# Third norm's scalar steps on GpSimd in place of VectorE, in a fused decoder layer

## The reference

```
x = x + attn(layernorm(x))      # q, k, v, o projections with LoRA, then a gated MLP
x = x + xattn(layernorm(x), ctx, ctx)
x = x + ffn(layernorm(x))

layernorm(x) = (x - mean(x)) / sqrt(var(x) + 1e-5)

xattn(Q, K, V):                 # per sequence and head
    corr = ifft(fft(q) * conj(fft(k))).real
    w, idx = top_k(corr, 8);  w = softmax(w)
    out = sum_i w_i * v[min(idx_i + pos, L - 1)]

ffn(x):                         # one of 8 LoRA experts for each token
    logits = x @ route_w.T;  best = top_1(logits)
    out = (one_hot(best) * logit)[..., None] * (x @ A.T) @ Bw
```

## Time and profile before

| | |
|---|---|
| median of 3 runs | 811.79 us |
| profiled execution, own time | 812.52 us |
| its span, first to last instruction | 810.3 us |
| TensorE busy | 753.6 us, 93% |
| VectorE busy | 563.3 us, 70% |
| ScalarE busy | 420.7 us, 52% |
| GpSimd busy | 242.3 us, 30% |
| mean granted TensorE clock | 0.983 |

### The profile page before, as it was taken

One profiled execution on the slowest core, in us unless ns is written; L12 is line 12 of the kernel. 1 busy time (PEld: TensorE's weight loads), 2 busy tenths in 40 slices (PEclk: granted clock), 3 DMA queues, 4 the chain that ended last, 5 costly groups with the idle time before them and its releaser, 6 DMA issues.

```text
span 810.3 us, 10362 instructions
## 1 busy us (share of the span) xinstructions
PE 753.6 (93%) x3256; PEld 532.3 (66%) x3256; DVE 563.3 (70%) x1291; ACT 420.7 (52%) x759; POOL 242.3 (30%) x196
## 2 busy tenths in 40 slices
PE   3979999999999999999999999999997778999975
PEld 1335778777888888888888888887774233444432
DVE  5998874567897477557637647752346689999983
ACT  7794753655664354345445435431132456777651
POOL 0001221033363343243343334321111142444441
PEclk9999999999999999999999999999999899999997
DMA  7463210012323023112302301120231535556301
GB/s 208 147 247 135 73 52 1 1 40 66 117 79 105 14 65 104 40 37 81 90 14 81 102 14 55 49 72 2 65 82 49 133 93 153 157 157 170 105 26 40
DMA packets 31286, 67.27 MB, mean 83 GB/s; under 512 B 4800, under 2 KB 5184, under 8 KB 31232
## 3 DMA queue, kind: packets, MB, share of 16 engines
q1 hardware_dynamic: 31232, 66.60, 27.6%
HBM read 45.61 MB, written 4.19 MB: 61 GB/s over the span
## 4 chain that ended last, share of the span: by engine, by line
PE 65%; issue 14%; DVE 9%; POOL 8%; ACT 3%; DMA 1%; SPq 0%; POOLq 0%; DVEq 0%; ACTq 0%
PE ps L667 19%; PE ps L669 19%; PE ps L668 19%; POOL pn L1120 5%; POOL en L1069 2%; PE ps L638 1%; POOL pw L850 1%; DMA lb<-in_lora_attn_b 1%; DVE piece_d L393 1%; DVE piece_c L389 1%; PE ps L463 1%; PE ps L462 1%; PE ps L693 1%; PE ps L898 1%; DVE odd_c L389 1%
## 5 line engine op out<-in xcount | busy, mean ns | idle before, releaser
L667 PE MATMUL ps<-x_hi,w_hi 128*128 128x512 f32 x448 | 176.2, 393 | 0.2 <-POOL w_lo L524 0.2
L669 PE MATMUL ps<-x_hi,w_lo 128*128 128x512 f32 x448 | 174.7, 390 | 0.0
L668 PE MATMUL ps<-x_lo,w_hi 128*128 128x512 f32 x448 | 174.3, 389 | 0.0
L783 POOL TENSOR_TENSOR h_lo<-hf,h_hi 128x512 fp32r<-128x512 f32 x56 | 74.0, 1321 | 244.5 <-ACT h_hi L778 244.4
L792 DVE TENSOR_TENSOR acc<-acc,ps 128x512 f32<-128x512 f32 x112 | 76.3, 684 | 73.1 <-PE ps L669 73.1
L771 DVE TENSOR_TENSOR hf<-hf,ps 128x512 f32<-128x512 f32 x56 | 38.4, 686 | 86.9 <-PE ps L669 86.9
L667 PEld LDWEIGHTS ps<-x_hi,w_hi 128*128 128x128 f32 x448 | 84.1, 188 | 21.6 <-issue 4.0
L524 POOL TENSOR_TENSOR w_lo<-wt,w_hi 128x512 fp32r<-128x512 f32 x42 | 62.4, 1486 | 113.8 <-ACT w_hi L517 113.8
L669 PEld LDWEIGHTS ps<-x_hi,w_lo 128*128 128x128 f32 x448 | 84.1, 188 | 18.0
L668 PEld LDWEIGHTS ps<-x_lo,w_hi 128*128 128x128 f32 x448 | 84.2, 188 | 17.3
L667 PE MATMUL ps<-w_hi,h_hi 128*128 128x512 f32 x224 | 88.1, 393 | 2.6 <-DVE acc L718 1.4
(11 more groups left out here) (153 smaller groups left out, 1324.9 us busy)
## 6 DMA issues: line engine op xcount, KB each, us to landing
codes_sb<-in_codes SPq DMA_DIRECT2D x40, 256.0 KB, 2.9
scale_sb<-in_scale_rows SPq DMA_DIRECT2D x80, 128.0 KB, 2.8
kc<-ku SPq DMA_DIRECT2D x64, 128.0 KB, 3.3
kx<-ku SPq DMA_DIRECT2D x32, 256.0 KB, 3.6
lft<-in_lora_ft SPq DMA_DIRECT2D x14, 512.0 KB, 4.3
acc<-in_x SPq DMA_DIRECT2D x4, 1024.0 KB, 8.2
ctx<-in_ctx SPq DMA_DIRECT2D x16, 256.0 KB, 4.9
out<-fin SPq DMA_DIRECT2D x16, 256.0 KB, 4.2
```

Of the source, the lines that this page charges most:

```text
L667: nc.tensor.matmul(bank, hi, rhs_hi, start=start, stop=False)
L668: nc.tensor.matmul(bank, hi, rhs_lo, start=False, stop=False)
L669: return nc.tensor.matmul(bank, lo, rhs_hi, start=False, stop=stop)
L783: nc.gpsimd.tensor_tensor(h_lo[:, c % 2, i], hf[:, i], h_hi[:, c % 2, i].bitcast(F32), ALU.subtract).then_inc(hlo_done, 1)
```

## The change

The four VectorE functions are gone, and GpSimd makes the same values behind its power, tile by tile. [...] Each waits for the step before it by the semaphore scaled3, which now counts six for a tile; the two waits on it (in dve_stats and in act_normalise_x3) change their numbers with it. In GpSimd's piece the two functions stand last in the slot, behind pool_pow.

```diff
@@ dve_stats
-            dve.wait_ge(scaled3, 4 * (t - 1))
+            dve.wait_ge(scaled3, 6 * (t - 1))
@@
-    def dve_square(dve, t, b):
-        dve.wait_ge(pow3, t + 1)
-        nc.vector.tensor_tensor(na3[:, b], pw3[:, b], pw3[:, b], ALU.mult).then_inc(scaled3, 1)
-
-    def dve_residual(dve, t, b):
-        dve.wait_ge(scaled3, 4 * t + 1)
-        nc.vector.scalar_tensor_tensor(out=nb3[:, b], in0=na3[:, b], scalar=-0.5, in1=ve3[:, b],
-                                       op0=ALU.mult, op1=ALU.mult).then_inc(scaled3, 1)
-
-    def dve_rstd(dve, t, b):
-        dve.wait_ge(scaled3, 4 * t + 2)
-        nc.vector.scalar_tensor_tensor(out=rs3[:, b], in0=nb3[:, b], scalar=1.5, in1=pw3[:, b],
-                                       op0=ALU.add, op1=ALU.mult).then_inc(scaled3, 1)
-
-    def dve_shift(dve, t, b):
-        dve.wait_ge(scaled3, 4 * t + 3)
-        nc.vector.scalar_tensor_tensor(out=nm3[:, b], in0=mv3[:, b, 0:1], scalar=-1.0, in1=rs3[:, b],
-                                       op0=ALU.mult, op1=ALU.mult).then_inc(scaled3, 1)
+    def pool_rstd(pool, t, b):
+        pool.wait_ge(pow3, t + 1)
+        nc.gpsimd.tensor_tensor(na3[:, b], pw3[:, b], pw3[:, b], ALU.mult).then_inc(scaled3, 1)
+        pool.wait_ge(scaled3, 6 * t + 1)
+        nc.gpsimd.tensor_tensor(nb3[:, b], na3[:, b], ve3[:, b], ALU.mult).then_inc(scaled3, 1)
+        pool.wait_ge(scaled3, 6 * t + 2)
+        nc.gpsimd.tensor_scalar(na3[:, b], nb3[:, b], -0.5, 1.5, ALU.mult, ALU.add).then_inc(scaled3, 1)
+        pool.wait_ge(scaled3, 6 * t + 3)
+        nc.gpsimd.tensor_tensor(rs3[:, b], na3[:, b], pw3[:, b], ALU.mult).then_inc(scaled3, 1)
+
+    def pool_shift(pool, t, b):
+        pool.wait_ge(scaled3, 6 * t + 4)
+        nc.gpsimd.tensor_tensor(nb3[:, b], mv3[:, b, 0:1], rs3[:, b], ALU.mult).then_inc(scaled3, 1)
+        pool.wait_ge(scaled3, 6 * t + 5)
+        nc.gpsimd.tensor_scalar(nm3[:, b], nb3[:, b], -1.0, None, ALU.mult).then_inc(scaled3, 1)
@@ act_normalise_x3
-        act.wait_ge(scaled3, 4 * (t + 1))
+        act.wait_ge(scaled3, 6 * (t + 1))
@@ GpSimd's piece
                 if a := at(4):
                     pool_pow(pool, *a[:2])
+                if a := at(4):
+                    pool_rstd(pool, *a[:2])
+                if a := at(4):
+                    pool_shift(pool, *a[:2])
@@ VectorE's piece, behind dve_hidden
-                if a := at(5):
-                    dve_square(dve, *a[:2])
-                if a := at(5):
-                    dve_residual(dve, *a[:2])
-                if a := at(5):
-                    dve_rstd(dve, *a[:2])
-                if a := at(5):
-                    dve_shift(dve, *a[:2])
```

## The result

The changed kernel takes 816.07 us (median of 5 runs, 814.92 to 819.25) against 811.79 us: ratio 1.0054, 95% interval 1.0031 to 1.0077. The forecast was 815.2 us. The profiled execution took 814.92 us, the fastest of the five, with a span of 813.1 us, 2.8 us over the span before.

What follows compares the result with a forecast made beforehand. TensorE and VectorE have no room in the third norm's stage; with the change Loop D sets the slot. Terms sum to +3.4 us: 815.9 on the profiled execution, 815.2 us on the median; 8-in-10 range 809.5 to 828 us.

Steps and rivals of the forecast that it cites:

- ordinary slots: Slots 5 to 13, 9.46 us each before; forecast 9.98 us each, +4.7 us for the nine.
- slot 3: Third slot: VectorE's four scale steps no longer meet GpSimd's pn, so their stall goes; 13.69 to 9.98 us, −3.7.
- slots 1 to 15: Stretches of the third norm's stage, each from one start of GpSimd's power to the next.
- the end: Behind the last power: power to normalise grows from about 0.82 to 1.66 us, partly beside the expert matmul; +0.7 us.
- Slot 1: First slot: VectorE's four statistics, and pc with them, come forward by 0.9 us; −1.0 us.
- Price of a step: Each added one-column GpSimd operation: 0.19 us plus 0.08 for the semaphore, 0.27 us; 1.62 us for six.
- The rival with twice VectorE's time: Added GpSimd steps cost 0.40 us, something like twice VectorE's 0.16 and the hand-over; +15.1, 826.9 us; chance 0.14.
- Loop D: Path over GpSimd: power, six steps, pn, en, then VectorE's wl to x3 and next power; longest, 9.98 us.
- Loop C: Two-slot path over ScalarE and TensorE: pc, power, six steps, normalise, wu; 9.84 us a slot.
- The rival in which the stall stays: In slot 3 the freed VectorE steps still meet pn or the small steps; 3.7 us stay, 818.9 us; chance 0.12.
- the small GpSimd steps beside them: In slot 3 these could hold up the four VectorE scale steps, 0.2 us each, 0.8 us, mostly hidden.
- Slots 2, 4, 14 and 15: Four-column power ahead of pn, +1.3; longer Loop D, +0.1; wl waiting for en, +1.0; late normalise, +0.3 us.

Runs made afterwards that it cites:

- b_plus_six: Kernel before, VectorE's four steps kept, plus six one-column GpSimd scratch steps behind the power, ahead of pn; 818.02 us, ratio 1.0068.
- a_eight_steps: Changed kernel with two more one-column GpSimd multiplies repeating the shift's product, same result; 826.57 us, ratio 1.0184.
- two-step kernel: Changed kernel without its Newton step, leaving only the two GpSimd steps of the shift behind the power; 807.30 us, ratio 0.9936.
- b_scale_head: Kernel before with only the second norm's four scale steps moved on VectorE from behind the shift to the head of its slot; 810.71 us, ratio 0.9973.
- b_guard: Kernel before with only a wait added, so that GpSimd starts pn behind VectorE's shift; 813.19 us, ratio 1.0000.
- a_six_behind: Changed kernel plus six GpSimd scratch steps a tile behind pn and en, in front of the next power; 816.57 us, ratio 1.0049.
- b_six_behind: Kernel before plus six GpSimd scratch steps a tile behind pn and en, in front of the next power; 820.95 us, ratio 1.0099.
- b_six_behind_guard: b_six_behind with one wait more: GpSimd starts pn only when VectorE's shift of the tile in front is done; 812.03 us, ratio 0.9982.

## Why the prediction was right

The time came out, 815.2 us forecast and 816.07 measured, and so did the mechanism of the ordinary slots and of slot 3. That the sum came so close is in part luck. The forecast terms, slots 1 to 15 and the end, add up to +3.4 us; in the profiled pair the same stretches measured +1.4. Slot 1 gave back 1.9 us more than forecast and the end 0.9 us more, and the ordinary slots lost 0.6 us more. The pair's +2.8 us contains 1.43 us ahead of the first power, for which the forecast has no term. Between the medians the difference is +4.3 us, and by the interval of the ratio it lies between 2.5 and 6.3.

- **Price of a step.** Taken as 0.19 and 0.08 us; measured 0.19 and 0.08 to 0.09. The memset and a read was the right neighbour; since a whole multiply takes 0.19 us, at least half of the power's constant 0.39 us belongs to the power alone. This was the term on which the sign hung, and its bounds were wide (0.18 to 0.47). The rival with twice VectorE's time falls: a one-column multiply takes 0.19 us on GpSimd against 0.15 to 0.16 on VectorE. The ratio of 1.96 in the Trainium skill (page "GPSIMD Engine Reference", section 3.1) is for 2048 columns and does not carry over to one column: here it is 1.2.
- **Loop D.** 9.98 us forecast, 10.04 measured. The path from the power to pn took 2.20 us instead of 2.12, as the power itself took 0.57 us and the last step 0.23. The rest of the loop kept its lengths: 2.41 us from wl to x3, 1.89 from x3 to the power. b_plus_six shows that the queue alone makes this slot, and a_eight_steps that steps count whole. Nine slots gave +5.3 us for +4.7 forecast.
- **Loop C.** The normalise did come late (0.75 us of waiting), and at 9.84 us by the sum this loop was close behind, but no ordinary slot shows it last: b_plus_six has the long slot without it, and in a_eight_steps every step counts whole. Below about 9.4 us TensorE's own work is the bound, as the two-step kernel shows.
- **Slot 3.** −3.7 forecast, −3.64 measured, and that the stall is the meeting of the scale steps with pn is shown by b_scale_head. The rival in which the stall stays falls; the small GpSimd steps beside them, for which the prediction allowed 0.8 us, did not hold them up. Not all of the stall is waiting on VectorE: before, TensorE stood idle for 3.07 us, the clock of the slot was 0.88, and the three groups behind the gap took 4.92 us; in b_guard, with a gap of 2.26 us and a clock of 1.00, they took 3.29. So some 1.6 us of it were the clock.
- **Slot 1, mis-sized:** −1.0 forecast, −2.85 measured. pc starts 3.40 us behind the power instead of 4.63, so 1.2 us come from the statistics, as argued. The rest goes with TensorE's clock, which the sum had left out. Before, TensorE stood idle for 3.11 us in front of the next transform, the granted clock of the slot was 0.88, and the matmuls behind the gap ran long; after, the gap was 0.97 us and the clock 1.00. TensorE before, and then changed:

```profile
655.12 1.55 PE L898 MATMUL ps<-ctx,spec 64*128 64x512 f32 x4 [3.11 <-DVE pc L1111]
656.60 1.97 PE L987 MATMUL ps<-pp,spec 128*64 128x512 f32 x4
658.36 1.41 PE L1133 MATMUL ps<-pc,spec 128*64 128x512 f32 x4
```

```profile
655.32 1.13 PE L895 MATMUL ps<-ctx,spec 64*128 64x512 f32 x4 [0.97 <-DVE pc L1108]
656.38 1.08 PE L984 MATMUL ps<-pp,spec 128*64 128x512 f32 x4
657.29 1.03 PE L1130 MATMUL ps<-pc,spec 128*64 128x512 f32 x4
```

  The three groups took 4.93 us before and 3.24 after, 1.7 us less. a_six_behind repeats it (11.03 us, clock 1.00), but two other kernels with the same order on VectorE do not: the eight-step kernel, with a gap of 2.50 us in front of the turn of xh and 0.51 in front of the transform, has a clock of 0.75 and 13.54 us, and the two-step kernel, with gaps of 0.86 and 2.29 us, a clock of 0.87 and 12.68 us. In the changed kernel and in a_six_behind the clock was low just ahead of the first power (0.82 and 0.83), where it was 1.00 in the kernel before and in these two. So the 1.7 us may be the same low stretch in another place, and are not shown to be a gain of the change; what decides where it falls is open.
- **Slots 2, 4, 14 and 15:** +1.3, +0.1, +1.0 and +0.3 forecast, +1.43, +0.15, +1.00 and +0.19 measured.
- **The end, missed:** +0.7 forecast, −0.18 measured. The granted clock in this stretch was 0.59 before and 0.67 after, and the last routing matmuls took 1.19 us instead of 2.18, while the expert matmul ahead of them took 2.08 instead of 1.13. The clock moves there by more than the term; whether the late normalise cost its 0.7 us cannot be read from it.

What the prediction did not see at all is that the kernel before stood at an edge, with the shift 0.01 to 0.02 us ahead of pn in slots 6 to 12. The change removes that edge too. It is not seen to matter for the result: in the profiled execution of before no ordinary slot lost by it, not even slot 13, where the two met, and b_guard, where they cannot meet, has the same time.

## What to carry to other kernels

An engine's idle time is worth something only where the moved instruction lands: the same six GpSimd steps cost 0.6 us a slot ahead of a late product and almost nothing behind it. Before moving work, add up the loops that pass through the new queue, with what is queued behind, and compare the longest with the slot. And look in the timeline for small VectorE steps with two SBUF inputs beside long GpSimd products; here, moving two lines to get them out of the way gained 0.3%, where the change lost 0.5%.

## What the runs showed of the hardware

- A VectorE step of 0.16 us with two SBUF inputs that starts 0.03 us behind a GpSimd product takes 1.25 us, to the end of that product; one that starts 0.01 us ahead takes 0.16. A hundredth of a microsecond is also as fine as the profile tells starts apart: in the kernel before one scale step (L555) stands 0.01 us behind pn and still took 0.15. The Trainium skill (page "SBUF — State Buffer", section "SBUF: two separate sides") describes this as an exclusive hold for the whole instruction by whoever starts first, and the trace agrees with it in these rows. Not expected was how it repeats: in b_six_behind the shift met pn in nine slots in a row, and seven of these took about 10.59 us.
- The wait may go the other way too: in b_six_behind_guard a one-column GpSimd multiply took 0.70 us instead of 0.19 where it started 0.02 us behind wl. No run tried it by itself.
- A chain of one-column GpSimd operations with a semaphore between them goes at 0.27 us a step, on VectorE at 0.19.
